# One convolution chunk of a Mamba-2 mixer done later: VectorE's three operations and ScalarE's silu on it move into the first rounds of the loop over heads

## The reference

```python
zxbcdt = jnp.einsum('bld,ed->ble', u, in_proj_w)            # u: rmsnorm of x
z, xBC, dt = jnp.split(zxbcdt, [D_INNER, D_INNER + CONV_DIM], axis=-1)
conv = conv_general_dilated(xBC_t, conv_w, window_strides=(1,), padding=[(3, 0)], ...)
xBC = silu(conv + conv_b)                                    # 1280 channels
x, Bm, Cm = jnp.split(xBC, [D_INNER, D_INNER + D_STATE], axis=-1)
dt = softplus(dt + dt_bias); dA = exp(dt * -exp(A_log))
# for each of 16 heads, token by token:
h = h * dA_t + dt_t * B_t * x_t ;  y = h . C_t
y = rmsnorm((y + D * x) * silu(z), ssm_norm_w)
out = einsum('ble,de->bld', y, out_proj_w)
```

## Time and profile before

| | |
|---|---|
| median of 3 runs | 2758.64 us (2756.23 to 2761.95) |
| the profiled execution | 2757.51 us, of which 2755.7 us is the span from the first to the last instruction |
| mean granted TensorE clock | 0.996 |
| PE busy | 2675.0 us, 97% |
| PEld busy | 2074.0 us, 75% |
| DVE busy | 1530.9 us, 56% |
| ACT busy | 1021.6 us, 37% |
| POOL busy | 670.6 us, 24% |
| one inner step of the mixer | 101.40 us |

### The profile page before, as it was taken

How to read it: one execution, slowest core, us unless ns; L and a number is a source line. 1 busy time by engine, 2 the same in 40 slices (tenths; PEclk the granted TensorE clock), 3 DMA queues, 4 the chain that set the end, 5 groups by cost and what they waited for, 6 DMA issues and landing times.

```text
span 2755.7 us, 42318 instructions
## 1 busy us (share of the span) xinstructions
PE 2675.0 (97%) x15264; PEld 2074.0 (75%) x15264; DVE 1530.9 (56%) x2561; ACT 1021.6 (37%) x2375; POOL 670.6 (24%) x594
## 2 busy tenths in 40 slices
PE   7999999999999999999999989999999998999999
PEld 5777777777778888888888867777777766777776
DVE  8797797788785331333133377777777773111122
ACT  6334334434434222122212255555555553222221
POOL 5553453463361100010001101332223321000000
PEclk9999999999999999999999999999999999999999
DMA  4101101101114101110112030111011123211111
GB/s 152 46 2 46 46 0 46 46 0 46 46 47 139 62 19 42 61 61 14 47 61 96 23 108 11 60 61 39 30 61 53 57 93 114 83 48 46 46 46 46
DMA packets 85482, 147.83 MB, mean 54 GB/s; under 512 B 4032, under 2 KB 17984, under 8 KB 85408
## 3 DMA queue, kind: packets, MB, share of 16 engines
q1 hardware_dynamic: 85408, 146.84, 15.3%
HBM read 113.27 MB, written 33.55 MB: 53 GB/s over the span
## 4 chain that ended last, share of the span: by engine, by line
PE 87%; DVE 8%; issue 2%; ACT 1%; DMA 1%; POOL 0%; DVEq 0%; SPq 0%; POOLq 0%; ACTq 0%
PE ps L75 22%; PE ps L77 22%; PE ps L76 22%; PE ps L1710 4%; PE ps L2071 4%; PE ps L780 3%; PE ps L1722 2%; DVE mx_cv L585 1%; PE ps L1701 1%; PE ps L756 1%; DVE at_pT L1573 1%; DVE mx_m L593 1%; PE ps L768 1%; PE ps L1730 1%; DVE at_r_hl L1580 1%
## 5 line engine op out<-in xcount | busy, mean ns | idle before, releaser
L1417 ACT ACTIVATE at_pr<-ps,at_nm 128x256 f32<-128x256 f32 x512 | 235.9, 473 | 191.7 <-DVE at_nm L1567 191.7
L1110 DVE TENSOR_TENSOR gm_m_lo<-gm_m,gm_m_hi 128x512 fp32r<-128x512 f32 (+1 forms) x88 | 61.0, 693 | 416.8 <-ACT gm_m_hi L1027 416.8
L75 PE MATMUL ps<-sh_u_hi,gm_gu_hi 128*128 128x512 f32 (+1 forms) x704 | 274.7, 390 | 1.6 <-DVE gm_gu_lo L227 1.6
L76 PE MATMUL ps<-sh_u_lo,gm_gu_hi 128*128 128x512 f32 (+1 forms) x704 | 274.6, 390 | 0.0
L77 PE MATMUL ps<-sh_u_hi,gm_gu_lo 128*128 128x512 f32 (+1 forms) x704 | 274.6, 390 | 0.0
L1573 DVE COPY at_pT<-ps 128x512 f32<-128x512 f32 x256 | 176.1, 688 | 127.4 <-PE ps L1710 124.1
L1021 ACT ACTIVATE gm_sg<-ps 128x512 f32<-128x512 f32 (+1 forms) x88 | 52.7, 598 | 518.4 <-PE ps L77 518.3
L75 PE MATMUL ps<-sh_u_hi,qm_w_hi 128*128 128x512 f32 x512 | 201.4, 393 | 0.0
L77 PE MATMUL ps<-sh_u_hi,qm_w_lo 128*128 128x512 f32 x512 | 199.4, 390 | 0.0
L76 PE MATMUL ps<-sh_u_lo,qm_w_hi 128*128 128x512 f32 x512 | 199.3, 389 | 0.0
L530 POOL TENSOR_TENSOR mx_m<-mx_m,mx_g 128x512 f32<-128x512 f32 x128 | 185.0, 1445 | 45.6 <-DVE mx_m L595 45.3
(11 more groups left out here) (252 smaller groups left out, 6331.1 us busy)
## 6 DMA issues: line engine op xcount, KB each, us to landing
sh_xf<-x_scratch SPq DMA_DIRECT2D x16, 1024.0 KB, 7.5
mx_xr<-in_x SPq DMA_DIRECT2D x8, 1024.0 KB, 5.9
h_scratch<-mx_xr SPq DMA_DIRECT2D x8, 1024.0 KB, 5.0
sh_xf<-h_scratch SPq DMA_DIRECT2D x8, 1024.0 KB, 8.2
gm_xr<-in_x SPq DMA_DIRECT2D x8, 1024.0 KB, 7.3
gm_r<-h_scratch SPq DMA_DIRECT2D x8, 1024.0 KB, 6.1
x_scratch<-gm_r SPq DMA_DIRECT2D x8, 1024.0 KB, 5.1
at_cf<-in_ctxT SPq DMA_DIRECT2D x16, 512.0 KB, 3.7
```

The costliest lines, as they stand in the source:

```text
L75: nc.tensor.matmul(out, l_hi, r_hi, start=first, stop=False)
L76: nc.tensor.matmul(out, l_hi, r_lo, start=False, stop=False)
L1417: A(pr[h][:, t, :], SC[h][:, SEQ * t:SEQ * t + SEQ], ACT.Exp, bias=nm[:, 4 * n + h, t:t + 1], accum_out=sums[:, 2 * b + t, 4 * g + h:4 * g ...
```

## The change

DVE's `conv(i, NCONV - 1)`, which stood between `scale_x(i, 0)` and the loop over heads, moves to the end of the loop's round 0, behind the product of that round. ACT's `silu(i, NCONV - 1)`, which stood ahead of the loop, moves into round 1, behind the square. ACT's `tap` of this chunk stays where it was. No instruction is added or removed, and no wait is changed.

```diff
@@ scalar, main
             silu(i, NCONV - 2)
             zsilu(i, 0)
             tap(i, NCONV - 1)
-            silu(i, NCONV - 1)
             for j in range(KI):
...
                 A(acc[:, :] if j == 0 else sq[:, :], zs[j % 2][:, :], ACT.Square).then_inc(s["gs"], 1)
+                if j == 1:
+                    silu(i, NCONV - 1)
                 if 1 <= j <= TT:
                     norm(i + 1, j - 1)
@@ vector, main
             scan(i, 0)
             scan(i, 1)
             scale_x(i, 0)
-            conv(i, NCONV - 1)
             if step_0(i):
                 wt.low(dve, IN_PIECES)
             for j in range(KI):
...
                 V.tensor_tensor(zs[j % 2][:, :], xc[:, j, :], zs[j % 2][:, :], ALU.mult).then_inc(s["g"], 1)
+                if j == 0:
+                    conv(i, NCONV - 1)
```

## The result

The changed kernel takes 2768.68 us (median of 8 runs, 2766.86 to 2769.22) against 2759.22 us before (8 runs, 2756.23 to 2764.16): ratio 1.0032, 95% interval 1.0023 to 1.0041. The medians are 9.5 us apart. The forecast was 2768.0 us.

The account below looks back on a forecast made before the run. PE was taken to bound the kernel (87% of the chain), DVE mattering only where PE waits. Terms 6.3 + 1.65 + 1.5 = 9.5 us gave 2767.0, plus 1.1 for the median: 2768 us, range 2765 to 2771 (8 in 10: 2759 to 2774).

Parts of the forecast that it names:

- The hole: Round 0: DVE idles 1.15 us before L678, which needs PE's unmoved chunk_y(0).
- What is late: Behind the moved convolution, scan(4) starts 0.93 us late and chunk_out(0) 0.9 us, per step.
- The 0.23 us that the product was to gain: Round 0: DVE's product takes 0.68 instead of 0.91 us, POOL's last product ending just before it.
- Which wait ends last: Round 1: PE idles some 1.4 us before turn_x(2), then some 0.3 before spread(7); 0.9 us is lost.
- Not given back: From round 2 on both engines run 0.9 us late with no further PE wait; seven steps, 6.3 us.
- Step 0: First step: L678 already waits for PE before the change, so scan(4) starts 1.65 us late.
- The last step: SP's four loads wait for the later silu, delaying ACT's conversion, zsilu(3) and turn_x(3); 1.5 us.
- The prediction's own lower bound: Last step's load term costs 0 if the first piece lands within 2.5 us of issue.
- clock rival: PE's idle time in round 1 drops its clock, about 3 us per round hit, 24 in all steps; chance 0.07.

Follow-up runs that it names:

- e2: Changed kernel with the whole last-chunk convolution moved to just in front of L678 in round 0, silu left in round 1; 2762.16 us, ratio 1.0012 to before.
- e3: Changed kernel with g_low(0) moved from round 1 to between the second and third operation of the moved convolution; 2770.82 us, ratio 1.0036 to before.
- e9: Changed kernel unaltered, run a third time; 2768.64 us, ratio 1.0038 to before.
- e7: Changed kernel unaltered, run again beside the kernel before on the same chip; 2768.62 us, ratio 1.0037 to before.
- e1: Changed kernel with only ACT's silu moved back, to the end of round 0; 2768.39 us, ratio 1.0030 to before.
- e4: Changed kernel with the last chunk's three convolution operations cut to 8 columns of each sequence, leaving out computation; 2755.34 us, ratio 0.9988 to before.
- e5: Kernel before with two convolution operations in front of L678 in round 0, the third behind scan(5), silu behind zsilu(2) in round 1; 2754.27 us, ratio 0.9987.
- e6: Changed kernel with the whole convolution moved on to behind scan(5) of round 1, silu unchanged; 2765.36 us, ratio 1.0027 to before.
- e10: Split convolution run again: against the kernel before, two operations in front of L678, the third behind scan(5), silu behind zsilu(2); 2755.39 us, ratio 0.9987.
- e11: Run again of the changed kernel with the whole convolution just in front of L678 in round 0; 2760.26 us, ratio 1.0009 to before.

## Why the prediction was right, point by point

**The hole.** Predicted 1.15 us in front of L678 in round 0; measured 1.07 as the engine's idle time is printed. By starts L678 stands at 269.19 - 2.47 = 266.72 against 266.71 predicted. e2 fills it and the cost of each step is gone.

**What is late.** Predicted: `scan(4)` 0.93 us late, `chunk_out(0)` 0.9 us, bounds 0.76 to 0.93. Measured 0.94 and 0.87. The 0.23 us that the product was to gain, because POOL would be done, came: it took 0.68 us. The rule of the Trainium skill ("SBUF — State Buffer", in "SBUF: two separate sides"), that two such operations exclude each other, wasn't called on, by a margin of 0.09 us. That margin was thin for a term worth 0.1 to 0.7 us a step: here the prediction was right with some luck. Elsewhere the trace bears the rule out more plainly than by the 0.91 us: in step 2 of the kernel before, `g_low(1)` starts at 277.64 and takes 1.50 us instead of 0.66, while POOL's sum of squares runs from 277.31 to 278.60.

**Which wait ends last.** Predicted 1.4 us ahead of `turn_x(2)` and 0.3 ahead of `spread(7)`, the second binding. Measured 1.45 and 0.38, and e3 shows that the second binds: with the first gone it grows to 1.24.

**Not given back.** Right: from round 2 on each inner step repeats the 0.85 us, with no further wait of PE.

**Step 0.** Predicted 1.65 us, measured 1.67 in the first pair of profiles (109.47 - 107.80), in which `scan(4)` starts at 68.71 where 68.81 was predicted. That close an agreement is luck. The other profiles of the changed kernel have 109.02 and 108.05 us, the other one of the kernel before 108.78, so any pair gives between -0.7 and 1.7 us, 0.6 in the mean. In e9 the hole isn't there at all in step 0: `scan(3)` is late too and L678 starts behind it with no wait.

**The last step: right in size, wrong in cause.** I predicted 1.5 us from SP's queue, because the loads wait for the later silu. The first profile seemed to bear it out: beyond the 0.85 us of every step, step 7 was 2.43 - 0.85 = 1.58 us longer than before. But its rows say something else. PE in step 7, by stretch (length, busy, instructions, clock, DMA share, GB/s):

```profile
787.00:789.00 2.00, 1.27 (x7) 1.00 0.00 0
789.00:791.00 2.00, 2.00 (x7) 0.61 0.00 0
791.00:793.00 2.00, 2.00 (x6) 0.54 0.00 0
793.00:795.00 2.00, 2.00 (x10) 1.00 0.86 261
```

and matmul by matmul:

```profile
788.95 0.39 PE L75 MATMUL ps<-mx_wout_hi,mx_g_hi 128*128 128x512 f32 x1
...
789.81 0.63 PE L75 MATMUL ps<-mx_wout_hi,mx_g_hi 128*128 128x512 f32 x1
...
793.29 0.39 PE L75 MATMUL ps<-sh_u_hi,mx_wz_hi 128*128 128x512 f32 x1
```

`chunk_out(0)` took 793.29 - 788.95 = 4.34 us where step 2 has 280.57 - 277.85 = 2.72: 1.62 us more. The granted clock was at 0.50, the 1.2 GHz level, in part of both middle windows (in 790 to 792 us it reads 0.50), and PE had been idle for 1.41 and 0.16 us shortly ahead of it. The loads came as predicted (SP issued them at 792.21), and ACT waited for them, but its conversion was done before PE's projection:

```profile
791.57 0.61 ACT L440 ACTIVATE mx_xc<-mx_cv 128x512 f32<-128x512 f32 x1
...
794.84 0.73 ACT L214 ACTIVATE gm_gu_hi<-gm_r,sh_post_w 128x512 fp32r<-128x512 f32 x1 [2.05 <-DMA gm_r<-in_gate_wT]
796.22 0.60 ACT L446 ACTIVATE mx_zs<-ps 128x512 f32<-128x512 f32 x1 [0.66 <-PE ps L77]
```

In e7 the clock held in that step, and ACT was last. Its ACT and PE:

```profile
794.76 0.72 ACT L214 ACTIVATE gm_gu_hi<-gm_r,sh_post_w 128x512 fp32r<-128x512 f32 x1 [2.11 <-DMA gm_r<-in_gate_wT]
795.39 0.58 ACT L446 ACTIVATE mx_zs<-ps 128x512 f32<-128x512 f32 x1
```

```profile
796.02 0.66 PE L758 MATMUL ps<-sh_ident,mx_xc 128*128 128x128 f32 x4 [0.15 <-ACT mx_zs L446]
```

So the later loads cost PE 0.15 us of idle time in e7 and 0.23 in e9, 0.2 to 0.3 us of the step, not 1.5; e1, where the loads are early, has a step 7 that is 0.25 us shorter than e7's. The term was mis-sized because I took the landing as 4.0 us, the median of four transfers issued together. The conversion needs only the first, and began 794.84 - 792.21 = 2.6 us after its issue in the changed kernel, 2.7 and 2.8 us in e7 and e9. The prediction's own lower bound (0 if the first piece lands within 2.5 us) was nearly the right case. That the sum came out at 9.5 us all the same is luck: this term was 1.2 us too large, step 0's in the mean 1.1 us, and time that the sum had no term for, read below, made up for it. The length of step 7 in the first profile alone would have confirmed a wrong story.

**What makes up the rest.** From the start of the first step to the end the changed kernel took 2743.6, 2743.5 and 2742.1 us in its three profiles, the kernel before 2734.1 and 2735.0: 8.5 us more in the mean. In the mean, with the rounding of each, the inner steps hold 6 x 0.86 = 5.2 of them, step 7 holds 1.5 (2.4, 1.1 and 1.2), step 0 holds 0.6, and the stages behind the mixer hold 1.3. Of this only the wait for `scan(5)`, 0.85 us in each of steps 1 to 7 or 6.0 us (6.3 predicted), and the 0.2 to 0.3 us of the loads are shown to come from the moved instructions. The medians differ by 9.5 to 11.1 us, another 1 to 2.6 us, and where those stand isn't shown.

The 1.3 us are at least partly clock. In all three profiles of the changed kernel the entry to the gated MLP, behind some 1.6 us of idle time, ran at half clock for a few microseconds, and in neither profile of before did. This is its first matmul in the changed kernel, to be set against the earlier trace rows:

```profile
844.20 0.77 PE L75 MATMUL ps<-sh_u_hi,gm_gu_hi 128*128 128x512 f32 x1 [1.63 <-DVE gm_gu_lo L227]
```

From that entry to the end the changed kernel took 1920.9, 1922.5 and 1921.9 us, the kernel before 1920.6 and 1920.4. It doesn't hang on the wait for `scan(5)`, though: the entry was hit in e1, e3, e4, e5, e6, e10 and e11 as well, and in e5, e10 and e11 PE has no such wait. And e11 is the same kernel as e2, in which the entry was not hit. What decides it isn't shown; no run was made on it.

The prediction had a clock rival, in round 1, at about 3 us for each round that is hit. It came true in one round of step 7 in one profile, at 1.6 us. In the 18 inner steps of the three changed profiles, each with the same wait of about 1.45 us, no such stretch fell there.

## What to carry to other kernels

An instruction that an engine runs between two waits for another engine may be filling a hole. Before it is moved, ask what the engine will do in the old place: if the next instruction depends on something that isn't moved with it, the hole opens and all the work behind it comes later by about its width. Half-fill such a hole only with what fits, and put the rest behind the last thing that the other engine needs (e5). And the largest wait printed isn't always the one that binds: take it away in thought and see which wait ends next (e3).

## What the runs showed of the hardware that I had not expected

- **Half clock is not tied to one wait.** The same 1.4 us wait of PE in round 1 was followed by 1.6 us lost at half clock in step 7 of one profile, and by none in the other 20 such rounds of steps 1 to 7 in the three profiles of that kernel.
- **Two profiles of one kernel differ by 4 us in places that nothing touched.** Before starts its first step at 21.60 us in one and at 24.68 us in another, and the spans are 2755.7 and 2759.7 us. The lengths of the steady steps repeat to 0.1 us (101.35 to 101.45 in both), which is why they, not spans, tell an effect of 1 us a step.
- **A short DVE operation costs more than its share.** The convolution's operation, each one waiting for the one before, takes 0.23 us from start to start on 16 columns (0.70 for three, e4) and 0.74 on 510: about a thirtieth of the columns for a third of the time. No size in between was run.
- **A wait can hide in a merged group.** In step 2 the 0.38 us for `scan(5)` showed only as 1.09 us instead of 0.71 for two matmuls.
